# Sixteen result tiles, each loaded as two halves of 64 partitions from two DMA queues

## The reference, cut to what matters

```
y   = silu(xg @ gate_w.T) * (xg @ up_w.T) @ down_w.T         # per expert and slot
out = zeros_like(flat).at[tok_table].add(y * w_table)          # four rows per token
out = out + shared_experts(flat)
x   = x + _layernorm(out)                                      # over the 256 features
```

## Time and profile before

| what | value |
|---|---|
| median of 3 runs | 1083.43 us (1081.32 to 1083.98) |
| the profiled execution's own time | 1083.0 us |
| its span, first to last instruction | 1081.3 us |
| TensorE busy | 1005.0 us (93% of the span) |
| VectorE busy | 783.5 us (72%) |
| ScalarE busy | 551.2 us (51%) |
| GpSimd busy | 393.4 us (36%) |
| HBM traffic over the span | 105 GB/s |

### The profile page before, as it was taken

How to read it: one execution, slowest core, us unless ns; L and a number is a source line. 1 busy time by engine, 2 the same in 40 slices (tenths; PEclk the granted TensorE clock), 3 DMA queues, 4 the chain that set the end, 5 groups by cost and what they waited for, 6 DMA issues and landing times.

```text
span 1081.3 us, 22284 instructions
## 1 busy us (share of the span) xinstructions
PE 1005.0 (93%) x8288; PEld 618.7 (57%) x8288; DVE 783.5 (72%) x1763; ACT 551.2 (51%) x1242; POOL 393.4 (36%) x605
## 2 busy tenths in 40 slices
PE   6999899899999999999999999999999999999776
PEld 3445546665545666664555666665555666667452
DVE  4888725778889765778889755788888636687525
ACT  3888621356888321456888321446888321432302
POOL 3476401142676011132676011142766001141652
PEclk9999999999999999999999999999999999999979
DMA  6889500003444000003444000003445704005657
GB/s 223 296 294 311 163 1 20 1 2 101 148 138 144 3 1 20 21 2 111 139 146 137 2 1 20 21 2 120 135 142 166 186 1 116 22 2 156 203 206 292
DMA packets 74748, 113.85 MB, mean 105 GB/s; under 512 B 6167, under 2 KB 64542, under 8 KB 73744
## 3 DMA queue, kind: packets, MB, share of 16 engines
q1 hardware_dynamic: 71952, 104.63, 30.8%
q0 software_dynamic: 1536, 3.60, 1.0%
q10 hardware_dynamic: 1152, 4.19, 1.0%
HBM read 93.60 MB, written 19.40 MB: 105 GB/s over the span
## 4 chain that ended last, share of the span: by engine, by line
PE 65%; DVE 14%; issue 7%; ACT 6%; POOL 5%; DMA 3%; SPq 0%; DVEq 0%; POOLq 0%; ACTq 0%
PE bank L992 25%; PE bank L1089 5%; PE bank L1182 4%; DVE hf L1933 3%; PE bank L1301 3%; PE bank L1199 2%; PE bank L1412 2%; PE bank L1104 2%; PE bank L1005 2%; PE bank L1349 2%; DVE nmax L2383 1%; PE bank L1361 1%; PE bank L1463 1%; POOL rs L1759 1%; DVE hf L1947 1%
## 5 line engine op out<-in xcount | busy, mean ns | idle before, releaser
L992 PE MATMUL bank<-uT,w_in 128*128 128x512 f32 (+1 forms) x584 | 272.8, 607 | 4.0 <-DVE hf L1947 3.3
L1933 DVE SCALAR_TENSOR_TENSOR hf<-bank,conv_w,hf 128x510 f32<-128x510 f32 (+2 forms) x224 | 162.6, 744 | 34.6 <-ACT nmax L1605 20.3
L992 PEld LDWEIGHTS bank<-uT,w_in 128*128 128x128 f32 (+1 forms) x584 | 102.7, 188 | 124.2 <-issue 92.5
L1759 POOL TENSOR_TENSOR rs<-ve,half 128x2 f32<-128x2 f32 x56 | 39.1, 698 | 273.9 <-DVE ve L2086 273.9
L1588 ACT ACTIVATE hf<-bank,conv_b,conv_w 128x512 f32<-128x512 f32 x128 | 99.1, 774 | 50.1 <-PE bank L992 49.6
L992 PE MATMUL bank<-uT,w_gu 128*128 128x512 f32 x224 | 98.5, 593 | 0.0
L1182 PEld LDWEIGHTS bank<-hf 64*64 64x64 f32 x2048 | 74.1, 133 | 37.2 <-issue 30.8
L1182 PE MATMUL bank<-hf 64*64 64x128 f32 (+3 forms) x2048 | 88.2, 304 | 7.4 <-POOL hf L1822 3.6
L1566 ACT ACTIVATE xc<-bank 128x512 f32<-128x512 f32 x44 | 26.3, 597 | 104.1 <-PE bank L992 77.0
L2383 DVE TENSOR_REDUCE nmax<-bank 128x2 f32<-128x256 f32 (+1 forms) x128 | 65.0, 553 | 13.5 <-PE bank L1403 13.2
L992 PEld LDWEIGHTS bank<-uT,w_gu 128*128 128x128 f32 x224 | 42.3, 190 | 47.9 <-issue 47.4
(11 more groups left out here) (356 smaller groups left out, 2199.2 us busy)
## 6 DMA issues: line engine op xcount, KB each, us to landing
hf<-cum_dram SPq DMA_DIRECT2D x32, 384.0 KB, 3.4
dec<-cum_dram SPq DMA_DIRECT2D x32, 384.0 KB, 4.0
tmp<-cum_dram SPq DMA_DIRECT2D x32, 384.0 KB, 3.5
x<-cum_dram SPq DMA_DIRECT2D x32, 384.0 KB, 4.0
y_dram<-xf SPq DMA_DIRECT2D x16, 512.0 KB, 6.1
w_in<-in_w_in SPq DMA_DIRECT2D x1, 3584.0 KB, 11.5
w_in<-in_w_egu SPq DMA_DIRECT2D x6, 512.0 KB, 9.1
w_in<-y_dram ACTq DMA_DIRECT2D x5, 512.0 KB, 9.5
```

Source lines behind the costliest of these rows:

```text
L992: mm = pe.matmul(plan[key][0:n, :], w[:, k, cols], uT[:, k, :], start=k == 0, stop=k == DC - 1)
L1759: pool.tensor_tensor(rs[:, cols], ve[:, cols], half[:, cols], ALU.pow).then_inc(rstd_ready.sem, 1)
L1933: ins = dve.scalar_tensor_tensor(d, x, conv_w[:, j, TAPS - 1 - s:TAPS - s], d, ALU.mult, ALU.add)
```

## The change

`load_results` gets a third argument, `side`, and loads 64 partitions of a tile: side 0 is partitions 0 to 63, side 1 is 64 to 127. ACT loads side 0 of all 16 tiles in order, SP side 1 of all 16. Both halves of a tile count on the same semaphore `yk_in[i]`, so TensorE waits for 32 in place of 16.

```diff
-        def load_results(eng, i):
-
-            eng.dma_start(yk[i].rearrange("p b d -> p (b d)"),
-                          y_dram[i * P * TOPK:(i + 1) * P * TOPK, :].rearrange("(p b) d -> p (b d)", b=TOPK))\
-                              .then_inc(yk_in[i], 16)
+        def load_results(eng, i, side):
+            lanes = slice(side * (P // 2), (side + 1) * (P // 2))
+            rows = slice((2 * i + side) * P * TOPK // 2, (2 * i + side + 1) * P * TOPK // 2)
+            eng.dma_start(yk[i][lanes, :, :].rearrange("p b d -> p (b d)"),
+                          y_dram[rows, :].rearrange("(p b) d -> p (b d)", b=TOPK)).then_inc(yk_in[i], 16)
...
-            for i in range(1, TOKENS // P, 2):
-                load_results(sp, i)
+            for i in range(TOKENS // P):
+                load_results(sp, i, 1)
...
-                    pe.wait_ge(yk_in[i], 16)
+                    pe.wait_ge(yk_in[i], 32)
...
-            for i in range(0, TOKENS // P, 2):
-                load_results(act, i)
+            for i in range(TOKENS // P):
+                load_results(act, i, 0)
```

## The result

The changed kernel takes 1093.0 us in the median of four runs (1091.05 to 1095.28), the kernel before 1083.39 us. The ratio is 1.0093, with a 95% interval of 1.0067 to 1.0119: slower by 0.9%, outside the forecast range.

The account below looks back on a forecast made before the run. The end was taken to hang on VectorE's wait for `stored[0]` behind SP's result loads, bound by the sum of bytes. 1083.0 + 0 + 0 - 0 + 0.4 = 1083.4 us, 1083.8 on the median's scale; range 1080.6 to 1089.0.

Parts of the forecast that it names:

- What bounds the kernel: At the tail, VectorE idles 2.80 us for `stored[0]`, whose store lands behind SP's last load; the sum of bytes bounds.
- Bytes and place in the queues: Result loads: each queue moves 4.19 MB as before, so at 407 GB/s the last load lands when it did; cost 0.
- More issues: ACT's and SP's queues: sixteen issues each, at 0.56 and 0.53 us, stay covered or are absorbed by VectorE's idle; cost 0.
- Order of arrival: Result tiles: tile 14 could start near 1069.8 in place of 1071.15, but VectorE is busy until later; gain 0.
- The rate of half tiles: Result loads: two halves together run nearly like one whole tile; +0.4 us, with bounds 0, +12.6 and +31.
- The rivals: Alternatives for the result-load stage: halves collide (0.20), store freed sooner (0.12), ACT's issues uncover (0.04).
- The collision: Result loads: DMA engines in step write one partition side at a time; up to +12.6 us, partial +4.8; chance 0.20.
- its formula: Collision's price: 8.39 MB at the lower rate against 20.6 us; 330 GB/s gives 25.4 us, +4.8.
- Its sign: Collision's mark in the result-load stage: a rate below 352 GB/s and the last landing at 1074 or later.
- The store freed sooner: SP's queue: SP's loads finish ahead, the first store goes sooner, up to 2.80 us gained, 1080.6 to 1083 us; chance 0.12.
- The sentence on serializing halves: Skill's rule on two transfers to disjoint partition halves, read for the result loads as cost and gain of 0.
- The estimate by the port rule: Result loads: 64 partitions reach 8 of 16 ports, 196 GB/s; if halves took turns, 43 us for the stage, +22.

Follow-up runs that it names:

- sixteen buffers: Sixteen output buffers in place of eight, so no finish waits for a store: on the kernel before 1081.63 us (0.9981), on the changed kernel 1089.1 us (1.0058).
- columns: Changed kernel, but each tile's two loads are cut by columns, all 128 partitions with 2 KB each: 1084.4 us, ratio to before 1.0006.
- every second partition: Changed kernel, but ACT loads the even partitions of each tile and SP the odd ones: 1084.19 us, ratio to before 1.0008.
- one queue with all halves: Changed kernel, but SP alone loads all 32 halves, for each tile 64 to 127, then 0 to 63: 1097.89 us, ratio 1.0135.
- two queues that alternate: Changed kernel, but even tiles on ACT, odd on SP, each as two halves: begun on the same side 1100.79 us, on opposite sides 1096.52 us.
- halves from contiguous `y_dram` alone: Changed kernel, but SP alone loads partitions 0 to 63 of each tile, half the bytes left out: 202 GB/s, time not compared.
- shorter turns: Changed kernel, but each half is cut into two loads of 32 partitions, 128 KB each: 275 GB/s, time not compared.
- set lags: Changed kernel plus one extra load ahead on each queue: 8 partitions of 8 KB 1097.21 us, of 4 KB 1092.2 us; control of 16 partitions 1095.01 us.

## Why the prediction was wrong

*What bounds the kernel.* Right. The prediction read that the end hangs on `stored[0]`, and that on SP's last load. After the change the same chain of 7.06 us stands behind the same wait, and with sixteen buffers the wait goes, which is worth 2.5 us before and at most 2.7 after. One detail was off: the store lands 0.3 us behind the last load of both queues, ACT's, in either kernel.

*Bytes and place in the queues, at cost 0.* The bytes are the same and the rate is not; this step leaned on the rate and falls with it.

*More issues, at cost 0.* Right in effect: the number of issues costs nothing (columns and every second partition have as many). The issue was mis-sized, 0.64 us in place of 0.53. The row for it had been there: a 64-partition load took 0.61 us in the expert stage.

*Order of arrival, gain 0.* Right. In the two kernels with the new order of arrival and the full rate, nothing is gained: 1.0006 and 1.0008.

*The rate of half tiles, at +0.4 us.* This is the step that failed. Both ends were named, 0 and +12.6 from the 253 GB/s of the expert stage (with +31 beyond), and I took +0.4, next to 0. Measured were 277 GB/s and +9.6 us on the median. Three reasons had moved me to the wrong end. "At nearly every moment both sides are being written": in the change it holds, as far as which queue holds what can tell, and the rate was 277 GB/s, not 407. So two sides written by two loads are not what one whole tile is. "In the expert stage there was one queue": one queue with all halves gave 229 and the change 291, but two queues that alternate gave 222 and 235, so the second queue by itself is worth nothing that can be told, and even with each on its side the rate is far from full. "The rows of `w_edn` lie 64 KB apart, so part of the dearness may be theirs": halves from contiguous `y_dram` alone ran at 202 GB/s, so the place of the partitions is enough of a cause by itself; whether the spacing adds to it wasn't tried. The nearest row in the trace was the right one to follow.

*The rivals.* The collision, at 0.20, is what happened, and its price was near: with the measured 277 GB/s its formula gives 30.3 - 20.6 = 9.7 us, where the profiled execution, from which the 277 come, lost 8.05, since the rate rose behind 1070 us. That the median lost 9.6 is chance. Its sign also came: a rate below 352 GB/s and a last landing behind 1074. What it told of the mechanism is only half shown. Shown is that loads on one side are slow and that alternating such loads between the sides hardly helps (229 against 202 GB/s). That the DMA engines keep step, and that this is the reason, was not shown: shorter turns and set lags changed nothing that can be told. The rise from 236 to some 300 GB/s within the stage would fit with engines that drift apart, but that is only argued, and the kernel with every second partition rose at the start too, from 337 to 415. Why two halves on opposite sides don't reach the full rate stays open. The store freed sooner didn't happen; the wait grew from 2.80 to 3.98 us.

*The sentence on serializing halves.* The Trainium skill's "Don't bother — they serialize" ("DMA: Bandwidth & Descriptors", Rules for kernel authors) was taken as a cost of 0 because the DMA engines were full already. The runs contradict that reading: with whole tiles 1083.39 us, with halves 1093.0. A busy share near 1 doesn't say that the rate is full; it was 1.04 at 202 GB/s. The estimate by the port rule, +22 us if the halves took turns, was too dear, but had the right sign, and its premise, that one side alone is slow, is borne out (202 GB/s); the change lies between it and 0.

## What to carry to other kernels

A load to partitions 0 to 63 alone ran at half rate here, 202 GB/s against 403, and giving the other half to a second queue restored only part of it. That 64 to 127 are slow too is an estimate: had they run at 403, halves that take turns on one queue would have given about 270 by these figures, and they gave 229. If a tile must be cut, cut it so that each piece reaches both sides of partition 64: by columns, or every second partition; neither cost time that can be told here (1.0006 and 1.0008). Don't take busy DMA engines for a full rate; look at the GB/s. And where VectorE waits "for issue" ahead of a step that reuses an output buffer, look at what stands in front of the store in its queue; spare buffers bought 0.2%.

## What the runs showed of the hardware that was not expected

- Halves from one queue that alternate between the sides run at 229 GB/s, hardly above one side alone, although a tile's two halves, one on each side, follow each other within 2.3 us at that rate.
- Partitions 32 to 95 run at 397 GB/s, so it is the middle at 64 that counts, not the number of partitions.
- The same 32 half-loads ran at 291 GB/s in the change and at 312 with sixteen output buffers. What sets the rate of the halves in one execution is open. The times tell less: the changed kernel's four runs spread by 4.2 us, the four of before by 2.7, but 25 runs of before in another set by 4.6.
- The issue of a load takes longer for 64 partitions of 4 KB, and not because the transfers are slow: 0.64 us each in the change, but 0.68 with every second partition, at 408 GB/s (SP's sixteen from 1045.83 to 1056.65, below), against 0.53 for whole tiles and 0.51 for 128 partitions of 2 KB.

```profile
1045.83 6.21 SPq L544 DMA_DIRECT2D w_in<-y_dram  x9
1052.08 2.62 SPq L544 DMA_DIRECT2D x_pad<-y_dram  x4
1054.74 1.91 SPq L544 DMA_DIRECT2D w_gu<-y_dram  x3
```

- The first output store, which stands behind SP's loads, landed 0.3 us behind ACT's last load, before (1071.4 and 1071.1) and after (1079.5 and 1079.2), though SP's own last load had landed 0.5 and 1.5 us ahead of it.
